# Values products of an attention layer: two column groups of 64, or four of 32

## What is computed

```python
scores = jnp.einsum('bihd,bjhd->bhij', q, k) * scale + bias
attn = jax.nn.softmax(scores, axis=-1)
y = jnp.einsum('bhij,bjhd->bihd', attn, v).reshape(B, T, H * D)   # this product
return y @ Wproj
```

## Time and profile before

| what | value |
|---|---|
| median of three runs | 1379.82 us |
| profiled execution | 1376.99 us |
| its span, first to last instruction | 1375.3 us |
| mean granted TensorE clock | 0.992 |
| attention turns | from about 94 us to 1100 us |
| MATMUL records of L927 (`values`) | 1024, 64 turns of 16 |

### The profile page before, as it was taken

How to read it: one execution, slowest core, us unless ns; L and a number is a source line. 1 busy time by engine, 2 the same in 40 slices (tenths; PEclk the granted TensorE clock), 3 DMA queues, 4 the chain that set the end, 5 groups by cost and what they waited for, 6 DMA issues and landing times.

```text
span 1375.3 us, 29939 instructions
## 1 busy us (share of the span) xinstructions
PE 1321.1 (96%) x10448; PEld 1109.3 (81%) x10448; DVE 1058.0 (77%) x3292; ACT 937.5 (68%) x2357; POOL 194.6 (14%) x564
## 2 busy tenths in 40 slices
PE   4789999999999999999999999999999799999998
PEld 2577888878888887888888888878887588999897
DVE  6968996998799699969996996999699665544542
ACT  5769885887689588858886885888588533333333
POOL 4612111111111111111110111111111200000000
PEclk8999999999999999999999999999999999999999
DMA  6552232323233232313232332324131221111100
GB/s 212 191 160 86 93 115 71 102 101 106 66 107 102 84 88 78 130 58 115 101 105 68 103 105 73 100 73 135 52 120 67 79 69 43 43 43 43 43 16 31
DMA packets 88327, 123.02 MB, mean 89 GB/s; under 512 B 8577, under 2 KB 74482, under 8 KB 88178
## 3 DMA queue, kind: packets, MB, share of 16 engines
q1 hardware_dynamic: 87858, 121.11, 27.6%
q10 hardware_dynamic: 320, 0.00, 0.0%
HBM read 101.69 MB, written 19.40 MB: 88 GB/s over the span
## 4 chain that ended last, share of the span: by engine, by line
PE 77%; ACT 12%; DVE 4%; issue 2%; DMA 0%; POOL 0%; SPq 0%; DVEq 0%; ACTq 0%; POOLq 0%
PE at L848 15%; PE at L861 10%; PE at L900 9%; PE at L927 8%; PE at L1580 7%; PE at L971 7%; PE at L1616 7%; ACT prob L1113 5%; PE at L938 2%; PE at L881 2%; PE at L892 2%; PE at L886 1%; ACT probT L1122 1%; ACT area_raw L1070 1%; PE at L955 1%
## 5 line engine op out<-in xcount | busy, mean ns | idle before, releaser
L1113 ACT ACTIVATE prob<-prob,low 128x512 f32<-128x512 f32 (+3 forms) x512 | 280.8, 551 | 115.8 <-DVE low L1267 115.8
L1267 DVE CUSTOM_DVE_ANT_0 prob<-at,mask 128x512 f32<-128x512 f32 (+3 forms) x512 | 219.8, 486 | 8.8 <-PE at L861 8.8
L848 PE MATMUL at<-w_hi,c_lo 128*128 128x386 f32 x512 | 189.4, 370 | 1.5 <-DVE area_raw L1212 1.5
L848 PE MATMUL at<-w_hi,c_hi 128*128 128x386 f32 x512 | 173.7, 339 | 0.0
L848 PE MATMUL at<-w_lo,c_hi 128*128 128x386 f32 x512 | 173.6, 339 | 0.0
L1280 DVE TENSOR_SCALAR prob<-prob,rec 128x512 f32<-128x512 f32 (+3 forms) x512 | 169.6, 395 | 4.5
L900 PE MATMUL at<-ident,prob 128*128 128x128 f32 x1280 | 165.6, 276 | 3.1 <-DVE low L1267 1.7
L927 PE MATMUL at<-probT,v 128*64 128x512 f32 (+3 forms) x1024 | 151.9, 438 | 4.4 <-DVE probT L1290 2.8
L900 PEld LDWEIGHTS at<-ident,prob 128*128 128x128 f32 x1280 | 143.5, 142 | 10.6 <-DVE yT_lo L1296 1.6
L927 PEld LDWEIGHTS at<-probT,v 128*64 128x64 f32 x1024 | 75.5, 136 | 83.8 <-issue 69.1
L1122 ACT ACTIVATE probT<-at 128x512 f32<-128x512 f32 (+1 forms) x256 | 130.2, 536 | 5.4 <-PE at L900 2.7
(11 more groups left out here) (225 smaller groups left out, 3221.9 us busy)
## 6 DMA issues: line engine op xcount, KB each, us to landing
area_w<-in_L_ffn_w SPq DMA_DIRECT2D x65, 1024.0 KB, 5.7
bias<-in_L_ffn_w SPq DMA_DIRECT2D x160, 32.0 KB, 4.6
x_in<-in_L_attn_x SPq DMA_DIRECT2D x8, 512.0 KB, 5.4
xr<-in_L_attn_x SPq DMA_DIRECT2D x8, 512.0 KB, 5.0
eo_d<-hidT SPq DMA_DIRECT2D x32, 128.0 KB, 1.8
x_d<-xr SPq DMA_DIRECT2D x8, 512.0 KB, 3.0
area_raw<-x_d SPq DMA_DIRECT2D x8, 512.0 KB, 4.0
out<-area_raw SPq DMA_DIRECT2D x8, 512.0 KB, 2.9
```

The source lines that it names most:

```text
L848: m = eng.matmul(bQ[n % 2][:, 0:W], a[:, (j // HP) % 2, k, n * P:(n + 1) * P], w[:, k, j % HP, :], start=start, stop=(k == KC - 1 and a is ...
L1113: eng.activation(sl, sl, ACT.Exp, scale=-1.0, bias=low[:, i:i + 1], accum_out=den[:, i:i + 1]).then_inc(exp_done.sem, 1)
L1267: eng.tensor_tensor_reduce(out=prob[s % 2][h][:, off[c]:off[c + 1]], in0=bC[i][:, at:at + (c + 1) * P], in1=mask[:, (NT - 1 - c) * P:T], s ...
```

## The change

The product of each block of keys is cut by 32 output dimensions instead of 64: four products of 128x32 weights, in place of two of 128x64. Groups 0 and 1 both stream `probT[0]`, groups 2 and 3 both stream `probT[1]`. Waits, semaphores, tiles and everything on the other engines stay as they are.

```diff
                     for kc in range(NT):
-                        for h in range(2):
-                            m = eng.matmul(bY[h * D:(h + 1) * D, kc * P:T], v[:, s % 2, kc, h * D:(h + 1) * D],
-                                           probT[h][:, offT[kc]:offT[kc + 1]], start=(kc == 0), stop=(kc == NT - 1))
+                        for j in range(GRP):
+                            rows = slice(j * E, (j + 1) * E)
+                            m = eng.matmul(bY[rows, kc * P:T], v[:, s % 2, kc, rows], probT[j * E // D][:, offT[kc]:offT[kc + 1]],
+                                           start=(kc == 0), stop=(kc == NT - 1))
                     m.then_inc(pe_y.sem, 1)
```

## The result

The changed kernel takes 1371.79 us (median of 17 runs, 1370.12 to 1379.02), the kernel before 1380.88 us in the same rounds (17 runs, 1376.92 to 1385.32). The ratio is 0.9935, interval 0.9922 to 0.9949: 0.65% faster, 9.1 us between the medians. Forecast were 1374.1 us and a gain of 5.7 us, with 4 to 7.5 us as the likely range of the gain; the difference of the medians lies above that range.

What follows compares the result with a forecast made beforehand. TensorE was taken to bound three turns of four: 16 turns at 0.15 us (2.4) and 31 at 0.105 (3.3) give 5.7 us, so 1371.3 profiled, 1374.1 as median; own range 1372 to 1376, final 1370 to 1378.5.

Steps and rivals of the forecast that it cites:

- What bounds the kernel: Chain of waits stays on TensorE in three turns of four; savings in values plus expert's product count only there.
- Gelu turns: The 16 turns with s % 4 = 2, with a Gelu on ScalarE; TensorE has 0.8 us to spare, gain nothing.
- Streaming: In the value product: each group still streams 1280 columns in two passes, 2.13 us before and after; gain 0.
- The seam: Between values and the expert's product: no change of group width any more, 3.30 to 3.15 us; gain 0.15 us.
- Entering: From the last L848 to the first product of values: costs the same with four groups of 32; gain 0.
- Instructions: Values' 16 more load-matmul pairs: fourth group starts late where TensorE's list waits; 0.045 us charged in 31 turns.
- The 62 ns for a matmul: Skill's sequencer cost at values: fourth group some 0.19 us late, waiting turns' gain gone; prediction held its load row against it.
- Hindrance between groups of the same stream: In values, groups streaming the same probT take turns: 2.13 us more, 1491 us in total; chance 6%.
- Slow supply: At values after a wait, instructions come twice as slowly, fourth group 0.18 us late: 1376.9 us; chance 10%.
- No difference: At the seam, 0.17 us not from width change, or VectorE's or ScalarE's chain takes the gain: 1379.8; chance 12%.
- More than forecast: Full 0.15 us in 47 turns (1372.7), or Gelu turns profit too, 63 turns (1370.3); 6% beyond 7.5 us.
- own range of 1372 to 1376: Whole kernel's median: range for the main forecast of 1374.1 us, a gain of 4 to 7.5 us, given 66%.

Runs made afterwards that it cites:

- breaking it: One full-width product added between values and the expert's product, in the changed kernel (1397.07 us) and in the kernel before (1396.58 us).
- turning it round: expert_output in two groups of 64 instead of four of 32, on the kernel before (1395.34 us) and on the changed kernel (1395.16 us).
- the later traces: The changed kernel without further edits, timed a second time (1371.08 us) and a third (1371.68 us).
- the edit: The changed kernel with only group 0 of the four value groups computed; one run, 1368.56 us.

## Why the prediction was right, and where its sum was off

**What bounds the kernel**: right. The chain stayed on TensorE with a break in each fourth turn, and the two kernels with four groups in some turns confirm it: 0.2 us more with Gelu turns alone, 6.9 less with the others.

**Streaming, gain 0**: right. Values to the expert's product is 2.15 to 2.17 us (655.31 to 657.46, 683.47 to 685.64), the 2.13 us of streaming and little else, and a quarter of the product takes no less than 3.11 us of the 3.16.

**The seam, 0.15 us**: right in cause and in size (3.30 to 3.15), shown by breaking it (0.01 us left) and by turning it round (4.03 against 4.17). Strictly 0.14 us are the seam and 0.01 the narrower groups inside values, which the prediction had at nothing.

**Entering, gain 0**: right, 0.27 us as before.

**Instructions, a charge of 0.045 us in 31 turns**: this term was wrong, it is 0. Turn 36, a waiting one, takes 3.16 like turn 38. The weight loads say why. PEld in turn 36 of the changed kernel, cuts of the timeline at 655.285, 655.43 and 655.455 us, and one over all eight loads of the first two passes (a cut shows what is under way at that time, merged):

```profile
655.28 0.11 PEld L928 LDWEIGHTS at<-probT,v 128*32 128x32 f32 x1 [0.32 <-issue]
...
655.32 0.14 PEld L928 LDWEIGHTS at<-probT,v 128*32 128x32 f32 x5
...
655.35 0.12 PEld L928 LDWEIGHTS at<-probT,v 128*32 128x32 f32 x3
...
655.28 0.19 PEld L928 LDWEIGHTS at<-probT,v 128*32 128x32 f32 x8 [0.32 <-issue]
```

All eight loads have started and ended within 0.19 us of the first, and the last three start from 0.07 us on. I had taken the 0.09 us of the earlier trace rows for the time in which four loads are supplied, one for each group. But with two groups the third and the fourth load are those for the second pass of groups 0 and 1. In turn 38 of the kernel before, where nothing waited, they come 0.05 us behind the first two as well (685.06 and 685.00). So they said nothing of supply. Only the first group runs ahead after a wait, here by 0.04 us; the others come together, as the second one did before. With 0.15 us in 46 turns (those between turn 1 and turn 63 that are not Gelu turns) the sum is 6.9 us, and 975.8 - 968.9 = 6.9 is what the later traces show.

**The 62 ns for a matmul**, which the Trainium skill gives for a sequencer without hardware decode ("TensorE: Matmul & The Clock Gate", section "Wait — 56ns, not 53.3ns?"): the trace shows no such cost here. The eight loads, each of which stands ahead of a matmul in the list, started within 0.08 us. By that rule the fourth group of a waiting turn would have begun 0.19 us late (an estimate, three times the page's 62 ns), and the turn would have been longer than turn 38 by about that; they differ by 0.01. The page states the cost for hardware decode off only, and no run here shows whether it is on.

**The rivals.** Hindrance between groups of the same stream: excluded, 2.80 us for group 0 alone and 2.80 with the others. (Its 1491 us adds 114 us to the profiled execution; on the median, as the other rivals are, it is 1494.) Slow supply: excluded by turn 36. No difference: excluded. More than forecast: of its two forms the full 0.15 us in all 47 turns (7.1 us) is what the turns show (6.9 us in 46 of them), and profit in the Gelu turns is excluded. The prediction gave a gain beyond 7.5 us only 6%, and the medians show 9.1. Part of that is not its mechanism: the turns gained 6.6 to 7.0 us, inside its 4 to 7.5. The median lies 2.3 us below the forecast, outside its own range of 1372 to 1376 by 0.2: 1.4 us for the charge (31 x 0.045) and 2.0 us that are in these medians and not in the seams, less 1.1 us because the kernel before came out slower than the three runs on which the forecast stood (1380.88 and 1379.82). The median lies inside the final range of 1370 to 1378.5. Without those 1.1 us it would have stood at 1370.7, close to the edge, so its place well inside is in part luck; that the seam gives 0.15 us a turn is not.

## What to carry to other kernels

Where products are packed by column groups, compare the width with that of the block before and behind, not only with the size of the product. Cutting finer buys no streaming time, but a run of blocks of one width has one way in and one way out: here 0.14 us for each seam, about 0.1 us of it standstill (0.20 us from the last value record to the next block with the seam, 0.09 without). And of such a saving only the turns count in which the chain of waits runs over the block; count them before multiplying.

## What the runs showed of the hardware

- Changing the width of column groups between blocks of plain float32 products costs about 0.14 us, and it does so in both directions: 64 to 32 (3.30 against 3.15 us, of which 0.01 stays with a full-width product between) and 32 to 64 (4.17 against 4.03).
- With equal widths the next block's products start group by group: three of them began at 653.22 us, while the one that stands ahead of them in the list, whose group was busy, began at 653.43 or later. The Trainium skill says that matmuls start in strict program order ("TensorE: Matmul & The Clock Gate", "The mechanism"); for different column groups this trace does not agree, if the groups are told rightly from the edit.
- A group of 32 columns streams as fast with three others beside it as alone (2.80 us to its last pass in both); the whole pair takes 3.11 us with one group in values and 3.16 with four, as the last group trails the first by 0.05.
- The clock's lower level, 1.2 GHz, shows up in the stretch before the turns in a share that differs from run to run (mean granted clock 0.94 and 0.84 in the first two traces, 0.80 to 0.94 in all). The first value product stands between 105.9 and 113.1 us, a spread of 0.5% of the whole time, nearly as much as was to be measured. It comes later at a lower clock on the whole, but not strictly (111.7 us at 0.85, 108.8 at 0.84), so the clock is not shown to be all of it.
